# A recommendation tower's last round: layers 1 to 3 taken tile by tile in F32 products instead of jointly in rounded ones

## What is computed

```
e = stack([tbl_0[ids[:, 0]], ..., tbl_25[ids[:, 25]]], axis=1)
combined = concatenate([dense[:, None, :], e], axis=1)
interactions = einsum('bnd,bmd->bnm', combined, combined)
z = concatenate([dense, interactions[:, TRIU_I, TRIU_J]], axis=1)
h = concatenate([z, dense], axis=1)
h = maximum(h @ W_top1 + b_top1, 0)
h = maximum(h @ W_top2 + b_top2, 0)
y = h @ W_top3
```

## Time and profile before

| what | value |
|---|---|
| median of 3 runs | 472.18 us (470.95 to 473.91) |
| the profiled execution | 471.37 us |
| its span, first to last instruction | 469.5 us |
| TensorE matmul busy | 417.1 us, 89% |
| TensorE weight loads busy | 392.8 us, 84% |
| VectorE busy | 338.4 us, 72% |
| ScalarE busy | 223.7 us, 48% |
| GpSimd busy | 396.2 us, 84% |
| mean granted TensorE clock | 0.967 |

### The profile page before, as it was taken

How to read it: one execution, slowest core, us unless ns; L and a number is a source line. 1 busy time by engine, 2 the same in 40 slices (tenths; PEclk the granted TensorE clock), 3 DMA queues, 4 the chain that set the end, 5 groups by cost and what they waited for, 6 DMA issues and landing times.

```text
span 469.5 us, 11728 instructions
## 1 busy us (share of the span) xinstructions
PE 417.1 (89%) x4210; PEld 392.8 (84%) x4210; DVE 338.4 (72%) x777; ACT 223.7 (48%) x727; POOL 396.2 (84%) x553
## 2 busy tenths in 40 slices
PE   0766969989999989998799969999699988999898
PEld 0766869889999979898798969999698978988786
DVE  5897897986888677885597657876678855956260
ACT  3853654536553535455254443545254552536152
POOL 7899999899989998998998998899899899899600
PEclk9988997999999989999899999999899998999999
DMA  7992225122212312231212312222122212121100
GB/s 213 263 227 83 78 80 168 51 75 77 78 44 79 83 39 86 74 82 43 80 45 74 87 40 80 51 77 74 45 82 74 83 43 80 41 80 41 35 2 0
DMA packets 20046, 36.82 MB, mean 78 GB/s; under 512 B 8109, under 2 KB 10677, under 8 KB 19994
## 3 DMA queue, kind: packets, MB, share of 16 engines
q0 software_dynamic: 8704, 17.84, 14.3%
q1 hardware_dynamic: 11290, 18.28, 13.7%
HBM read 36.09 MB, written 0.01 MB: 77 GB/s over the span
## 4 chain that ended last, share of the span: by engine, by line
POOL 55%; issue 28%; PE 6%; DMA 3%; ACT 3%; DVE 2%; SPq 1%; POOLq 1%; DVEq 0%; ACTq 0%
POOL rows L414 29%; POOL y_wide L403 25%; DMA vecs<-in_tbl 3%; PE turn_ps L489 2%; PE dots_ps L473 1%; DVE inter L889 1%; POOLq L402 1%; ACT dots_ps L686 1%; SPq L297 1%; PE turn_ps L554 1%; PE mlp_ps L563 1%; DVE onehot L836 1%; ACT t_hi L679 1%; PE dots_ps L554 1%; DVE t_lo L853 1%
## 5 line engine op out<-in xcount | busy, mean ns | idle before, releaser
L414 POOL DMA_INDIRECT rows<-in_tbl,idx_sb x272 | 261.9, 963 | 45.6 <-POOL y_wide L403 43.7
L836 DVE TENSOR_TENSOR onehot<-ids_sb,late_ps 125x1024 fp32r<-125x1024 int32 (+2 forms) x154 | 167.3, 1143 | 8.2 <-DMA ids_sb<-in_ids_by_round 4.5
L889 DVE COPY_PREDICATED inter<-mask,dots_ps 27x48 f32<-27x48 int32 x496 | 103.1, 208 | 63.0 <-ACT inter L703 44.2
L403 POOL MEMSET y_wide<- 64x448 f32 x272 | 134.2, 493 | 0.2
L703 ACT COPY inter<-dots_ps 27x64 f32<-27x64 f32 x496 | 99.4, 200 | 67.0 <-PE dots_ps L473 54.5
L473 PE MATMUL dots_ps<-vecs 128*64 128x54 f32 x1984 | 117.3, 224 | 1.5 <-ACT vecs L672 0.9
L473 PEld LDWEIGHTS dots_ps<-vecs 128*64 128x64 f32 x1984 | 113.3, 139 | 5.8 <-issue 2.1
L489 PE MATMUL turn_ps<-onehot,t_hi 125*128 125x256 f32 x378 | 103.6, 309 | 13.6 <-DVE vecs L652 10.3
L489 PE MATMUL turn_ps<-onehot,t_lo 125*128 125x256 f32 x378 | 98.3, 295 | 0.0
L489 PEld LDWEIGHTS turn_ps<-onehot,t_hi 125*128 125x128 f32 x378 | 77.5, 205 | 18.5 <-issue 8.5
L489 PEld LDWEIGHTS turn_ps<-onehot,t_lo 125*128 125x128 f32 x378 | 77.5, 205 | 0.2
(11 more groups left out here) (86 smaller groups left out, 371.8 us busy)
## 6 DMA issues: line engine op xcount, KB each, us to landing
ids_sb<-in_ids_by_round SPq DMA_DIRECT2D x25, 384.0 KB
rows<-in_tbl,idx_sb POOLq DMA_INDIRECT x272
vecs<-in_tbl SPq DMA_DIRECT2D x8, 448.0 KB
rows<-in_r_dense_features SPq DMA_DIRECT2D x16, 64.0 KB
h_sb<-in_W_top_laid SPq DMA_DIRECT2D x2, 512.0 KB
vecs<-in_tbl SPq DMA_DIRECT2D x1, 560.0 KB
w_sb<-in_W_top SPq DMA_DIRECT2D x1, 512.0 KB
vecs<-in_tbl SPq DMA_DIRECT2D x8, 52.0 KB
```

What stands on the lines that cost most here:

```text
L403: pool.memset(unread, 0.0).then_inc(pauses_made, 1)
L414: nc.gpsimd.indirect_dma_start(out=rows[v % 2][:, s, :], out_offset=None, in_=tables[f - 1][:, :], in_offset=bass.IndirectOffsetOnAxis(ap= ...
L836: dve.tensor_tensor(part_buffer(k, h)[0:KP, 0:n], home.rearrange("p (o r) -> p o r", o=1).to_broadcast([KP, n, R]), row_of[KT[k]][0:KP, a: ...
L889: dve.copy_predicated(inter_of(u, q, g, a, n), mask[g * 32:g * 32 + N, a:a + n].rearrange("p (j s) -> p j s", s=1).to_broadcast([N, n, QS] ...
```

## The change

It is in the last round alone. Layer 1's inputs are no longer split there. Its products take the weights `w_hi` and `w_lo`, bitcast to F32, against `inter` and the dense block as they are, F32 too: two products of a block instead of three. ScalarE copies the dense block in the right order to `end_dense` (`place_dense`), which lies with the rectified values in `rows[0]`, free by then.

The two tiles go apart. Tile 2's layer 1 is 128 columns wide and stands between the last groups of transposes, in two halves of two output parts each, where the unread transposes stood. Tile 3's layer 1 goes by units of 64 columns, with layer 2 of tile 2 between the units. Layers 2 and 3 are taken for each tile by itself, 128 columns wide. Layer 3 of the round before moves ahead of the last transposes, and its copy of y with it. All unread transposes are gone. The second unit of dot products of tile 3 now waits until tile 2 is rectified, since both use `late_ps`.

```diff
-        end_h2_sb = rows[0][:, 0:M2 * R // D, :].rearrange("p s d -> p (s d)").rearrange("p (m r) -> p m r", r=R)
+        end_first_ps = [row_ps[:, m * P:(m + 1) * P] for m in range(M1)]
+        end_h2_ps = [[mlp_ps[0][:, 0:P], mlp_ps[0][:, P:2 * P]], [mlp_ps[0][:, 0:P], row_ps[:, 0:P]]]
+        end_h1_sb, end_dense, end_h2_sb = [
+            rows[0][:, a:b, :].rearrange("p s d -> p (s d)").rearrange("p (m r) -> p m r", r=r)
+            for a, b, r in ((0, M1 * 2, R), (M1 * 2, M1 * 2 + 2, P), (M1 * 2 + 2, M1 * 2 + 2 + M2 * 2, R))]
...
-            def end_of_layers(i):
-                parts, before = i * 8 + 8, i * (2 * M1) + M1
-                pe.wait_ge(x_hi_made, parts - 1)
-                pe.wait_ge(x_lo_made, parts - 1)
...
-                for m in range(M1):
-                    for n, (w, x) in enumerate(((w_hi, x_hi), (w_lo, x_hi), (w_hi, x_lo))):
-                        pe.matmul(end_ps[m], w[:, JG, m * P:(m + 1) * P], x[:, JG, :], start=(n == 0), stop=False)
-                stay_busy(mlp_ps[1], 14)
-                for m in range(M1):
-                    for at in range(3 * JG):
-                        if at < 2 * JG:
...
-                        last = pe.matmul(end_ps[m], w[:, jj, m * P:(m + 1) * P], x[:, jj, :],
-                                         start=False, stop=(at == 3 * JG - 1))
-                    last.then_inc(h1_done, 1)
-                pe.wait_ge(y_kept, i * 2 + 1)
-                for ks in (range(M1 - 1), (M1 - 1,)):
+            def end_layer1(i, v, u, bank_of_part, *ms):
+                cols = slice(0, P) if u is None else slice(u * (P // UNITS), (u + 1) * (P // UNITS))
+                units = v * UNITS + (UNITS if u is None else u + 1)
+                pe.wait_ge(inter_by_act, i * (4 * NA) + units * PER_UNIT)
+                pe.wait_ge(inter_by_dve, i * (4 * ND) + units * PER_UNIT)
+                pe.wait_ge(x_hi_made, i * 8 + 4 + v - 1)
+                for m in ms:
+                    for w in (w_hi, w_lo):
+                        for jj in range(JG + 1):
+                            last = pe.matmul(bank_of_part(m)[:, cols], w[:, jj, m * P:(m + 1) * P].bitcast(F32),
+                                             inter[:, jj, cols] if jj < JG else end_dense[:, v - 2, cols],
+                                             start=(w is w_hi and jj == 0), stop=(w is w_lo and jj == JG))
+                    if u != 0:
+                        last.then_inc(h1_done, 1)
+            def end_layer2(i, v, banks):
+                before = i * (2 * M1) + M1 + (v - 2) * M1
+                mine = slice((v - 2) * P, (v - 1) * P)
+                for ks in (range(M1 - 1), (M1 - 1,)) if v == 3 else (range(M1),):
                     for m in range(M2):
                         for k in ks:
                             pe.wait_ge(relu1_done, before + k + 1)
-                            last = pe.matmul(mlp_ps[m], w2_sb[:, k, m * P:(m + 1) * P], h1_sb[:, k, :],
+                            last = pe.matmul(banks[m], w2_sb[:, k, m * P:(m + 1) * P], end_h1_sb[:, k, mine],
                                              start=(k == 0), stop=(k == M1 - 1))
                         if M1 - 1 in ks:
                             last.then_inc(h2_done, 1)
+            def end_layer3(i, v):
+                mine = slice((v - 2) * P, (v - 1) * P)
                 for k in range(M2):
-                    pe.wait_ge(relu2_done, i * (2 * M2) + M2 + k + 1)
-                    last = pe.matmul(end_ps[0][0:1], w3_sb[:, k:k + 1], end_h2_sb[:, k, :],
+                    pe.wait_ge(relu2_done, i * (2 * M2) + M2 + (v - 2) * M2 + k + 1)
+                    last = pe.matmul(mlp_ps[1][0:1, mine], w3_sb[:, k:k + 1], end_h2_sb[:, k, mine],
                                      start=(k == 0), stop=(k == M2 - 1))
-                last.then_inc(y_done, 1)
+                if v == 3:
+                    last.then_inc(y_done, 1)
+            def end_of_layers(i):
+                end_layer1(i, 3, 0, lambda m: end_ps[m], *range(M1))
+                pe.wait_ge(y_kept, i * 2 + 1)
+                end_layer2(i, 2, end_h2_ps[0])
+                end_layer1(i, 3, 1, lambda m: end_ps[m], *range(M1))
+                end_layer3(i, 2)
+                end_layer2(i, 3, end_h2_ps[1])
+                end_layer3(i, 3)
 
...
                 layer1(i, 0, 3)
                 transpose_rows(i, 3, (2,))
                 layer2(i, 0, 0)
-                stay_busy(row_ps, 32)
+                layer2(i, 0, 1)
+                end_layer1(i, 2, None, lambda m: end_first_ps[m], 0, 1)
                 transpose_rows(i, 3, (3,))
-                layer2(i, 0, 1)
-                stay_busy(row_ps, 4)
+                layer3(i, 0)
+                end_layer1(i, 2, None, lambda m: end_first_ps[m], 2, 3)
                 transpose_rows(i, 3, (4,))
                 dots(i, 3, 0)
+                pe.wait_ge(relu1_done, i * (2 * M1) + 2 * M1)
                 dots(i, 3, 1, last_dots_ps)
-                layer3(i, 0)
                 end_of_layers(i)
...
-                if u == 0 and not (static(i) and i == 0 and v == 0):
+                if u == 0 and i * 4 + v not in (0, 2 * ROUNDS - 1):
                     act.wait_ge(x_lo_made, i * 8 + v * 2)
...
+            def place_dense(i, v):
+                act.wait_ge(*taken(turn_of["rows", i * 4 + v, 0]))
+                nc.scalar.copy(end_dense[:, v - 2, :].rearrange("p (h two s) -> p h two s", two=2, s=QS),
+                               in_turn(vecs[1][:, v - 2, :, 0])).then_inc(x_hi_made, 1)
+            def end_rectify1(i, v, bank_of_part):
+                mine = slice((v - 2) * P, (v - 1) * P)
+                for m in range(M1):
+                    act.wait_ge(h1_done, i * (2 * M1) + M1 + (M1 if v == 2 else M1 + m + 1))
+                    nc.scalar.activation(end_h1_sb[:, m, mine], bank_of_part(m)[:, 0:P], ACT.Relu,
+                                         bias=b1_sb[:, m:m + 1]).then_inc(relu1_done, 1)
+            def end_rectify2(i, v, banks):
+                mine = slice((v - 2) * P, (v - 1) * P)
+                for m in range(M2):
+                    act.wait_ge(h2_done, i * (2 * M2) + M2 + (M2 if v == 2 else M2 + m + 1))
+                    nc.scalar.activation(end_h2_sb[:, m, mine], banks[m], ACT.Relu,
+                                         bias=b2_sb[:, m:m + 1]).then_inc(relu2_done, 1)
...
                 rectify1(i, 0, 1, 2)
                 take_products(i, 2, 1)
                 take_vectors(i, 3, 1)
+                place_dense(i, 2)
                 rectify1(i, 0, 3)
-                split_input(i, 2)
-                act.wait_ge(*taken(turn_of["rows", i * 4 + 3, 0]))
-                split_dense(i, 3)
+                rectify2(i, 0, 0, 1)
                 take_vectors(i, 3, 3)
-                rectify2(i, 0, 0, 1)
+                place_dense(i, 3)
+                end_rectify1(i, 2, lambda m: end_first_ps[m])
                 take_products(i, 3, 0)
                 take_products(i, 3, 1, last_dots_ps)
-                split_input(i, 3, False)
-                for m in range(M1):
-                    act.wait_ge(h1_done, i * (2 * M1) + M1 + m + 1)
-                    nc.scalar.activation(h1_sb[:, m, :], end_ps[m], ACT.Relu, bias=b1_sb[:, m:m + 1]).then_inc(relu1_done, 1)
-                for m in range(M2):
-                    act.wait_ge(h2_done, i * (2 * M2) + M2 + m + 1)
-                    nc.scalar.activation(end_h2_sb[:, m, :], mlp_ps[m], ACT.Relu,
-                                         bias=b2_sb[:, m:m + 1]).then_inc(relu2_done, 1)
+                end_rectify2(i, 2, end_h2_ps[0])
+                end_rectify1(i, 3, lambda m: end_ps[m])
+                end_rectify2(i, 3, end_h2_ps[1])
...
                 merge_products(i, 2, 0)
                 merge_products(i, 2, 1)
                 take_vectors(i, 3, 0, 2)
-                split_input(i, 2)
-                split_dense(i, 3)
+                keep_y(i, 0)
                 take_vectors(i, 3, 4)
                 merge_products(i, 3, 0)
                 merge_products(i, 3, 1, last_dots_ps)
-                keep_y(i, 0)
-                split_input(i, 3, False)
-                keep_y(i, 1, end_ps[0])
+                keep_y(i, 1, mlp_ps[1])
```

More of the change, by code:

```diff
@@ L163, in dlrm_tower @@
         assert M1 == len(end_ps)
-        end_h2_sb = rows[0][:, 0:M2 * R // D, :].rearrange("p s d -> p (s d)").rearrange("p (m r) -> p m r", r=R)
+        end_first_ps = [row_ps[:, m * P:(m + 1) * P] for m in range(M1)]
[3 more added lines that the diff above has]
+            for a, b, r in ((0, M1 * 2, R), (M1 * 2, M1 * 2 + 2, P), (M1 * 2 + 2, M1 * 2 + 2 + M2 * 2, R))]
+        assert M1 * 2 + 2 + M2 * 2 <= NR
         ident_set = sem("ident_set")
@@ L530, in layer3 @@
                 last.then_inc(y_done, 1)
-            def end_of_layers(i):
-                parts, before = i * 8 + 8, i * (2 * M1) + M1
-                pe.wait_ge(x_hi_made, parts - 1)
-                pe.wait_ge(x_lo_made, parts - 1)
```

(27 more changed lines are left out.)

## The result

The changed kernel takes 486.12 us (median of 4 runs, 483.96 to 488.06), the kernel before 471.56 (4 runs, 470.27 to 473.91): a ratio of 1.030, 95% interval 1.024 to 1.036. It is slower by 14.6 us; 13.9 on the profiled execution and 486 for the median had been forecast. The profiled execution of the changed kernel took 488.06 us with a span of 486.3, the slowest of its four.

What follows compares the result with a forecast made beforehand. TensorE was taken to have slack before 443.99 and alone set the end after 456.71. A start 4.99 us late, an end stretch 9.3 longer and a tail 0.35 shorter sum to 13.9: forecast 486 us, own range 483 to 489.

Steps and rivals of the forecast that it cites:

- What bounds the kernel, and the slack before 443.99: Last 40 us: TensorE has free slack before 443.99, held by the last gather, and alone sets the end after 456.71.
- part 1: Before the last rows: 14.2 us of work in a cover of 9.2, so the last transposes start 4.99 us late.
- The price of a product: New products of layers 1 and 2: two records each, set by the weight load, 0.118 us a record, 0.236 a product.
- Part 2: Beside TensorE: the changed work of ScalarE and VectorE costs nothing; rectifications finish over 2.5 us before they are needed.
- Parts 3 and 4: From unit 0's last merge to the end of layer 2's stream: 23.2 us instead of 13.89, 9.3 longer.
- Part 5: Behind layer 2's stream to the end of the span, 3.47 us before: about 0.35 less, from narrower rectifications and layer 3.
- The sum: Whole change: 4.99 + 9.3 - 0.35 = 13.9 us, giving 485.3 for the profiled execution and 486.1 for the median.
- A: New TensorE records: loads are hidden, only streams count, 0.109 and 0.056 us a record; 475.2 us; chance 0.08.
- B: Layer 1: a new product is one record costing its stream only, 0.06 or 0.03 us; 465.3 us; chance 0.03.
- C: TensorE's clock falls to half over a third of the 160 late records, adding 5.3 us; 491.4 us; chance 0.06.
- D: TensorE: a load does not overlap the stream before it, together 21.7 us more; 508 us; chance 0.02.

Runs made afterwards that it cites:

- e4: The changed kernel, with tile 2's layer 1 cut to 8 products instead of 40 ahead of the last transposes; 479.25 us.
- e2: The changed kernel, with 9 of 10 products of each output part of tile 3's layer 1 streaming 16 columns instead of 64; 503.16 us, one run.
- e3: The changed kernel, with 8 of 10 products of each output part of tile 3's layer 1 loading 64 weight columns instead of 128; 479.89 us, one run.
- e1: The changed kernel, with tile 3's layer 1 in one run of 128 columns instead of two units of 64; 479.35 us.
- e6: The kernel before, with the last round tile by tile in rounded products, tile 3 in one run, no unread transposes; 470.80 us against 470.26, ratio 1.0013.
- e8: The same kernel as e6, run once more; 473.12 us against 472.10 for the kernel before, ratio 1.0007.
- e5: The kernel before, without the 50 unread transposes of its last round; 473.10 us against 471.78, ratio 1.0023.

## Why the prediction was right, and where it was off

- **What bounds the kernel, and the slack before 443.99** (e4): right. With the work cut to fit, the start comes back to its rows, 4.45 us earlier, where part 1 had 4.99. What did not hold is "what lies earlier stays as it is": in the profiled execution layer 2 starts 4.14 later than before (below).
- **The price of a product** was the term that carried all, and its form was right in each part: two records (the 40 products of a unit are x40 and x40 in the chain, 4.61 + 4.47 = 9.1 us for 80 records), a record set by the load (e2, e3), the same for 128 and 64 columns (e1). Its size was 0.112 us and not 0.118. The step that mis-sized it took twice the dot products' 0.058 and the 256-column record's 0.12. The latter is not bound by the load alone: the same rounded products over 128 columns take 0.112 (e6). Over 272 records this is 1.6 us too much. The Trainium skill, "TensorE: Matmul & The Clock Gate", section "LDWEIGHTS (loading the stationary operand)", gives the load as its columns over 1.2; the estimate from it, 107 ns for 128 columns, lies 5 ns below the 0.112 measured, where mine lay 6 above it.
- **Part 1, the start 4.99 late**: from layer 2's start to the last transposes it was 452.96 - 438.92 = 14.04 us, forecast 14.20. The records were cheaper (4.46 instead of 4.72 for each half), but at the four changes from one kind of product to another 0.07 to 0.10 us came in each time, 0.36 in all, which the sum had at nothing.
- **Part 2, nothing from ScalarE and VectorE**: it held behind the dot products: the four rectifications run from 453.17 to 454.31, and the second unit does not wait. It did not hold ahead of layer 2, where the prediction had looked at no wait: TensorE stood idle for 2.28 us ahead of 438.92 (above), until ScalarE had rectified the last part (from 438.29 on). ScalarE had a hole of 1.5 us amid its copies of tile 2's products, and the new copy of the dense block, 0.3 us, stands ahead of that rectification:

```profile
432.47 1.76 ACT L718 COPY inter<-dots_ps 27x64 f32<-27x64 f32 x8 [2.25 <-PE dots_ps L479]
435.70 1.78 ACT L718 COPY inter<-dots_ps 27x64 f32<-27x64 f32 x8 [1.47 <-remote]
437.50 0.59 ACT L667 COPY vecs<-turn_ps 128x512 f32<-128x512 f32 x1
437.99 0.41 ACT L732 COPY rows<-vecs 128x128 f32<-128x128 f32 x1
438.29 0.48 ACT L755 ACTIVATE h_sb<-mlp_ps,small 128x256 f32<-128x256 f32 x1
```

- **Parts 3 and 4, the end**: unit 0's last merge ends at 457.00 + 3.79 = 460.79, the last layer 2 product at 483.02 + 0.11 = 483.13. That is 22.3 us, where 13.9 stood before and 23.2 were forecast. The cheaper records are worth 192 x 0.006 = 1.2 less, the changes from one kind of product to another 0.3 in all more. That unit 1 has no wait was right.
- **Part 5**: the stretch behind layer 2 was forecast at 3.1 and is 486.3 - 483.13 = 3.2.
- **The sum**: from layer 2's start to the end 47.4 us against 469.5 - 434.78 = 34.7 before, so +12.7 and not +13.9. The cheaper record is -1.6 of the difference, the changes between kinds of product are +0.7, and -0.3 is a stretch that the sum took as unchanged: from the last transposes to unit 0's last merge it was 8.14 before (443.99 to 452.13) and 7.83 now (452.96 to 460.79). The remaining 4.1 us of the 16.8 by which the two spans differ lie ahead of that start. In the medians it is 14.6 - 12.7 = 1.9 us. So that 486 was met by 486.12 is in part luck. The parts that the sum is about came out 1.2 us under it, mostly by a record 5% too dear; 1.9 came in from elsewhere; and the kernel before was 471.56 in the median of four runs, 0.6 under the 472.18 from which the forecast was counted.

What of the later start is drift and what the new code? One and the same kernel varies by 4.7 us in it (e6 and e8 in the table, on two chips). Between the kernel before and the changed one most of the 4.14 us is there before any new code runs: the first dot products of tile 2, ahead of which the two programs are the same, start 2.83 apart. Kernel before:

```profile
419.34 3.75 PE L473 MATMUL dots_ps<-vecs 128*64 128x54 f32 x64
```

Changed kernel:

```profile
422.17 3.75 PE L479 MATMUL dots_ps<-vecs 128*64 128x54 f32 x64
```

Part of that is the clock in the seventh round, where it falls in the wait for rows: in the changed kernel's trace the dot products at 394.30 still take 4.57 us, where these two take 3.75. Columns as in the earlier trace rows, first the kernel before, then the changed one:

```profile
390.00:395.00 5.00, 5.00 (x53) 4.87 (x52) 4.92 (x5) 0.62 (x1) 4.51 (x7) 0.73 0.20 52
395.00:400.00 5.00, 5.00 (x56) 4.78 (x52) 2.67 (x14) 3.62 (x17) 4.51 (x7) 1.00 0.44 135
```

```profile
390.00:395.00 5.00, 4.73 (x25) 4.51 (x25) 4.01 (x5) 0.59 (x1) 4.51 (x8) 0.50 0.17 39
395.00:400.00 5.00, 5.00 (x70) 4.94 (x70) 2.44 (x9) 1.61 (x9) 4.51 (x7) 0.89 0.46 133
```

The other 1.31 us come in with the wait for ScalarE, of which 0.3 is the copy of the dense block. ScalarE's hole at that place is 1.2 to 1.5 us long in the changed kernel, e1, e2 and e3. It does not follow the new order: e5, whose program up to there is that of the kernel before, has it with 1.14 us, and e4, which has the new order, has none. No experiment was made on it, and what causes it is open.

What is shown, though, is what the drift does. In e5, with its cover unfilled, a start 1.7 us late leaves the last transposes at 444.46, 0.5 later than in the earlier trace rows, where the rows hold them. With the cover full a late start arrives at the end in full: the dot products follow 14.99 us behind layer 2 in all four traces with the whole of tile 2 in the cover, wherever it starts between 435.32 and 438.92. And e8's span is 4.5 us longer than e6's, its start 4.7 later.

The rivals: A (only the streams count) fell with e1 and e2. B (one record) fell with the records of the changed trace. C (the clock) did not come about at 64 columns, but its mechanism is real (e2, e5). D (load and stream in turn) fell at once: its 0.18 and 0.23 a record were 0.112, and a load of 192 ns in the records overlaps its neighbours. The Trainium skill, "TensorE: Matmul & The Clock Gate", section "The mechanism", says two things on it. Its list, which the prediction quotes, lets a load overlap a running product only where their row groups differ; these rows do not agree, since every load here fills all 128 rows. Its first paragraph, which the prediction leaves out, also lets a load go ahead where it goes to the background weight buffer; the 0.112 does not speak against that.

## What to carry to other kernels

Count a product of TensorE by its records and its weight columns before its streamed columns: over 128, 64 or 16 streamed columns a record with 128 weight columns took the same 0.112 us here, at full clock, so that splitting a layer into units pays for the weights again, and saves at most the wait that it hides (1.7 us for 9 here). At 256 streamed columns the stream counts again (0.216 us for an F32 record, in "The price of one product"). Two unrounded F32 products are four loads, three rounded ones three. And filler that nobody reads marks slack, not a free place of any size: measure the time from the first work in it to what ends it (9.2 us here, of which some 4 were taken already), and remember that the slack also takes up the drift of whatever runs before it.

## What the runs showed of the hardware

- The granted clock can fall with TensorE never idle. In e2, with 16 columns in nine of ten products, it went from 1.00 to 0.50 between 461 and 462 and stayed there until 499; with 64 columns, at the same 0.112 us a record, it stayed at 1.00.
- At half clock a record that its 128 weight columns bind takes nearly twice as long as well: 0.213 to 0.215 us instead of 0.112 (e2).
- Switching between 64 and 128 weight columns costs about 0.15 us at each change (e3, from 64 to 128: from 458.20 to 459.03 it is 0.83 us for eight records at 0.058 and two at 0.112, which alone would be 0.69).
- A steady row of transposes, 128 weight and 128 streamed columns each, keeps 0.109 us a record and so stays under the products' 0.112; its load records are 140 ns long and not 192.
